# Two residual layers chosen per batch row: the opening of the kernel on TensorE's side rewritten, and one copy at its end moved

## The reference

```
w = weights[subjects]; b = bias[subjects]
out = einsum('bct,bcd->bdt', x, w) + b[:, :, None]
x = x + out
H = einsum('btd,od->bto', x, W)
delta = einsum('btr,bor->bto', einsum('btd,brd->btr', x, A[idx]), Bm[idx]) * scalings[idx]
x = x + H + delta
```

## Time and profile before

| | |
|---|---|
| median of 3 runs | 241.67 us (241.47 to 241.75) |
| the profiled execution | 241.36 us |
| its span in the trace | 239.6 us |
| TensorE matmul / weight load busy | 229.4 us (96%) / 187.7 us (78%) |
| VectorE, ScalarE, GpSimd busy | 149.2, 107.9, 79.6 us |
| DMA | 36.64 MB, mean 153 GB/s |

### The profile page before, as it was taken

One profiled execution on the slowest core, in us unless ns is written; L12 is line 12 of the kernel. 1 busy time (PEld: TensorE's weight loads), 2 busy tenths in 40 slices (PEclk: granted clock), 3 DMA queues, 4 the chain that ended last, 5 costly groups with the idle time before them and its releaser, 6 DMA issues.

```text
span 239.6 us, 9653 instructions
## 1 busy us (share of the span) xinstructions
PE 229.4 (96%) x2900; PEld 187.7 (78%) x2901; DVE 149.2 (62%) x259; ACT 107.9 (45%) x185; POOL 79.6 (33%) x277
## 2 busy tenths in 40 slices
PE   1899999999999999999999999999999999999992
PEld 1787878888887888888888888888788888888761
DVE  6799848873358636875258835875448754425762
ACT  3184663543436363562436354454435434344441
POOL 4467771700077610610056730525135131000000
PEclk9999999999999999999999999999999999999998
DMA  5956455736565474645555574645646364562233
GB/s 132 279 169 193 141 176 156 198 94 176 148 197 141 120 213 131 201 108 192 134 154 163 147 215 109 192 115 160 172 135 191 109 200 110 155 178 63 83 78 90
DMA packets 23723, 36.64 MB, mean 153 GB/s; under 512 B 6162, under 2 KB 6162, under 8 KB 23698
## 3 DMA queue, kind: packets, MB, share of 16 engines
q1 hardware_dynamic: 16480, 26.10, 40.0%
q10 hardware_dynamic: 7218, 10.23, 13.7%
HBM read 19.53 MB, written 16.78 MB: 152 GB/s over the span
## 4 chain that ended last, share of the span: by engine, by line
PE 89%; DVE 2%; DMA 2%; ACTq 2%; issue 1%; ACT 1%; DVEq 0%
PE ps L883 69%; PE ps L843 14%; PE ps L819 3%; DMA o_ring<-in_L_cond_W_dram 2%; PE ps L764 1%; ACTq L693 1%; PE ps L775 1%; DVE o_ring L554 1%; ACT x_hi L658 1%; ACT m_f L681 1%; DVE x_lo L534 0%; PE ps L813 0%; DVE last_parts L539 0%; PE ps L871 0%; DVE o_ring L549 0%
## 5 line engine op out<-in xcount | busy, mean ns | idle before, releaser
L883 PE MATMUL ps<-m_hi,x_hi 128*128 x244 | 97.0, 398 | 0.0
L883 PE MATMUL ps<-m_hi,x_lo 128*128 x244 | 95.1, 390 | 0.0
L883 PE MATMUL ps<-m_lo,x_hi 128*128 x244 | 95.1, 390 | 0.0
L534 DVE TENSOR_TENSOR x_lo<-x,x_hi 128x512 fp32r<-128x512 f32 x64 | 44.7, 698 | 62.8 <-ACT x_hi L658 62.4
L374 POOL COPY p_pair<-p_all 64x64 f32 x128 | 42.8, 335 | 113.8 <-DVE x L526 96.9
L658 ACT ACTIVATE x_hi<-x 128x512 fp32r<-128x512 f32 x64 | 40.4, 632 | 56.0 <-ACT o_ring L671 30.9
L671 ACT ACTIVATE o_ring<-ps 128x512 f32<-128x512 f32 x60 | 35.9, 598 | 52.1 <-PE ps L883 50.7
L883 PEld LDWEIGHTS ps<-m_hi,x_hi 128*128 128x128 f32 x244 | 45.8, 188 | 10.7 <-issue 0.4
L883 PEld LDWEIGHTS ps<-m_hi,x_lo 128*128 128x128 f32 x244 | 45.8, 188 | 9.7
L883 PEld LDWEIGHTS ps<-m_lo,x_hi 128*128 128x128 f32 x244 | 45.8, 188 | 9.0
L526 DVE TENSOR_TENSOR x<-ps,bias_pair 128x512 f32<-128x512 f32 x64 | 43.6, 685 | 11.1 <-PE ps L843 10.1
(11 more groups left out here) (102 smaller groups left out, 82.4 us busy)
## 6 DMA issues: line engine op xcount, KB each, us to landing
x_ring<-in_x_dram SPq DMA_DIRECT2D x122, 128.0 KB, 2.7
out_dram<-o_ring ACTq DMA_DIRECT2D x64, 128.0 KB, 2.6
out_dram<-o_ring SPq DMA_DIRECT2D x64, 128.0 KB, 2.3
a_f<-in_L_cond_A_dram SPq DMA_DIRECT2D x8, 128.0 KB, 2.7
x_ring<-in_x_dram ACTq DMA_DIRECT2D x6, 128.0 KB, 3.4
o_ring<-in_L_cond_W_dram SPq DMA_DIRECT2D x2, 256.0 KB, 4.7
o_ring<-in_L_cond_W_dram ACTq DMA_DIRECT2D x2, 256.0 KB, 5.8
b_nat<-in_L_cond_Bm_dram ACTq DMA_DIRECT2D x1, 256.0 KB, 3.7
```

Source lines behind the costliest of these rows:

```text
L534: nc.vector.tensor_tensor(x1_lo[:, u % HELD], x1[:, u % 2], x1_hi[:, u % HELD], ALU.subtract).then_inc(x1_lo_ready, 1)
L883: mm = nc.tensor.matmul(ps[:, 2 + u % 2, :], part, m_tile(m, k, c), start=(c == 0 and part is hi and m is m_hi), stop=(c == TC - 1 and par ...
```

## The change

The edits, in the order of the program:

- The bias is no longer spread by DMA. GpSimd zeroes a tile `bias_row` of 128 x 512, SP loads the bias into its first row, TensorE multiplies it from the left by the 128 x 128 tile of ones (four fp32 products of 128 columns into bank 0), and ScalarE copies the bank to `bias_all`. SP's load of it stands between W's first and second block, and waits for the zeroing.
- `w` is loaded before W's first block.
- TensorE gets three bf16 products of 512 columns whose result nobody reads (`keep_busy`), between the counting products and the sum of the order. The first turn of W's block 0 moves behind the tables.
- ScalarE zeroes the rows of `a_parts` for the first adapter, GpSimd those for the second, behind the fourth pair.
- SP loads both halves of pairs 2 and 3; ScalarE loads those of pairs 0 and 1 only, with one table word read at a time.
- ScalarE copies chunks 0 to 2 of `wt`, VectorE chunk 3, behind its split of A. ScalarE rounds A of the second adapter behind its load of pair 7.
- Layer 0 of pair 3 moves behind layer 1 of pair 0. At the end, ScalarE copies the first row's low part of the last pair between the copies and the store of the pair before.

```diff
         def _(sp):
...
+            sp.dma_start(p_all[0:C], w.rearrange("s c d -> c s d")).then_inc(w0_in, 16)
             sp.dma_start(w_nat[:, 0, :], W[0:P, :]).then_inc(w_in[0], 16)
-            sp.dma_start(p_all[0:C], w.rearrange("s c d -> c s d")).then_inc(w0_in, 16)
+            sp.wait_ge(bias_zeroed, 1)
+            sp.dma_start(bias_row[0:1, :], bias.rearrange("s d -> (s d)").rearrange("(a n) -> a n", a=1)).then_inc(bias_in, 16)
             sp.dma_start(w_nat[:, 1, :], W[P:2 * P, :]).then_inc(w_in[1], 16)
...
-            b = words(sp, regs[:5], batch[0:1, 2:7], B - 1)
-            for i in range(1, XR):
-                load_half(sp, i, 0, b[2 * i - 2], x_first[i])
+            b = words(sp, regs, batch[0:1, 0:2 * XR], B - 1)
+            load_half(sp, 1, 0, b[2], x_first[1])
+            for i in range(2, XR):
+                load_x(sp, i, b[2 * i:2 * i + 2], x_first[i])
             load_a(1, 1)
             load_quad(XR)
...
-            for half in range(2):
-                nc.gpsimd.memset(a_parts[GR - GR * half:P - GR * half, half, :].bitcast(F32), 0.0).then_inc(rows_zeroed, 1)
-                pool.wait_ge(rows_zeroed, half + 1)
+            nc.gpsimd.memset(bias_row[:], 0.0).then_inc(bias_zeroed, 1)
...
-                    pool.wait_ge(bias_in, 16)
+                    pool.wait_ge(bias_ready, 1)
...
+                if n is None and j == HEAD - 1:
+                    pool.wait_ge(pair_ready, j * 4 + 4)
+                    nc.gpsimd.memset(a_parts[0:GR, 1, :].bitcast(F32), 0.0).then_inc(rows_zeroed, 1)
...
-            dve.wait_ge(wt_turned, 1)
-            nc.vector.tensor_copy(wt[:, 0, :], ps[:, FIRST, :]).then_inc(wt_copied_too, 1)
             a_split(0, 0)
+            dve.wait_ge(wt_turned, TC)
+            nc.vector.tensor_copy(wt[:, TC - 1, :], ps[:, FIRST + TC - 1, :]).then_inc(wt_copied_too, 1)
             x1_add(0, 0)
...
-            act.dma_start(bias_all[:], bias.rearrange("s d -> (s d)").rearrange("(a n) -> a n", a=1)
-                          .to_broadcast([P, S * C]).rearrange("p (s d) -> p s d", s=S)).then_inc(bias_in, 16)
...
+            def copy_last_low(j, u):
+
+                act.wait_ge(out_ready, j)
+                with act.If_ne(last_places[MIXED - 1][0], last_places[MIXED - 1][1]):
+                    copy_low_half(j, u, 0)
...
+            nc.scalar.activation(a_parts[GR:P, 0, :].rearrange("p (c k) -> p c k", c=TC), ones[GR:P, :].unsqueeze(1)
+                                 .to_broadcast([GR, TC, P]), ACT.Copy, scale=0.0).then_inc(rows_zeroed, 1)
             act.wait_ge(batches_ready, 1)
-            b = words(act, last_regs, batch[0:1, 0:2 * XR], B - 1)
-            for i in range(XR):
-                load_half(act, i, 1, b[2 * i + 1], x_first[i])
+            b, = words(act, regs[:1], batch[0:1, 1:2], B - 1)
+            load_half(act, 0, 1, b, x_first[0])
+            act.wait_ge(bias_spread, 1)
+            nc.scalar.activation(bias_all[:].rearrange("p s d -> p (s d)"), ps[:, 0, :], ACT.Copy).then_inc(bias_ready, 1)
+            b, = words(act, regs[1:2], batch[0:1, 3:4], B - 1)
+            load_half(act, 1, 1, b, x_first[1])
             a_round(0, 0)
+            copy_wt(0)
             copy_wt(1)
             copy_wt(2)
-            copy_wt(3)
...
-            a_round(1, 1)
             x1_round(1, 1)
             act.wait_ge(l0_done, XR)
             load_x(act, XR - 1, b, x_in)
+            a_round(1, 1)
...
                     copy_low(j, u)
+                    if j == PAIRS - 2:
+                        copy_last_low(j + 1, u + 1)
                     store_odd(j, u, last_batches[2 * n_of_mixed(j) + 1])
...
+            def spread_bias(part):
+
+                cols = slice(part * P, part * P + P)
+                return nc.tensor.matmul(ps[:, 0, cols], ones[:], bias_row[:, cols], start=True, stop=True)
+
+            def keep_busy(bank, times):
+
+                for _ in range(times):
+                    nc.tensor.matmul(ps[:, bank, :], ident_b[:], ident_b[:].unsqueeze(1).to_broadcast([P, TC, P]),
+                                     start=True, stop=True)
+
+            keep_busy(FIRST, 3)
...
-            for j in range(1, L0_QUAD):
+            for j in range(1, L0_QUAD - 1):
                 first_inputs(j)
                 layer0(j, j)
...
                     layer1_first(k[0])
+                    first_inputs(L0_QUAD - 1)
+                    layer0(L0_QUAD - 1, L0_QUAD - 1)
```

More of the change, by code:

```diff
@@ L671, in copy_out, with copy_low_half @@
                 nc.scalar.activation(o_ring[:, u % OR, :], ps[:, 2 + u % 2, :], ACT.Copy).then_inc(out_ready, 1)
+            def copy_low_half(j, u, half):
+                i = n_of_mixed(j)
+                act.wait_ge(low_done[half][i], 1)
+                nc.scalar.activation(low[0:C, half], ps[C:2 * C, 2 + 2 * half + u % 2, :],
+                                     ACT.Copy).then_inc(low_ready, 1)
             def copy_low(j, u):
@@ L678, in copy_low @@
                 with act.If_ne(last_places[i][0], last_places[i][1]):
-                    for half in range(2):
-                        act.wait_ge(low_done[half][i], 1)
-                        nc.scalar.activation(low[0:C, half], ps[C:2 * C, 2 + 2 * half + u % 2, :],
-                                             ACT.Copy).then_inc(low_ready, 1)
+                    for half in range(2) if j < PAIRS - 1 else (1,):
+                        copy_low_half(j, u, half)
                 with act.Else():
@@ L783, in _ @@
             nc.tensor.matmul(ps[:, 6, 0:K], ones[0:1, :], scal_row[:], start=True, stop=True).then_inc(scal_spread, 1)
-            pe.wait_ge(w_in[0], 16)
-            for c in range(TC):
-                turn_w(0, c)
+            pe.wait_ge(bias_in, 16)
+            for part in range(2):
+                spread_bias(part)
             pe.wait_ge(place_ready, 1)
@@ L794, in _ @@
             mm.then_inc(others_tabled, 1)
+            for part in range(2, TC):
+                mm = spread_bias(part)
+            mm.then_inc(bias_spread, 1)
+            pe.wait_ge(w_in[0], 16)
+            for c in range(TC):
+                turn_w(0, c)
+            turn_b(0)
             pe.wait_ge(w_in[2], 16)
@@ L807, in m_product_first @@
             def m_product_first(chunk):
-                if chunk == 0:
+                if chunk == TC - 1:
                     pe.wait_ge(wt_copied_too, 1)
                 else:
-                    pe.wait_ge(wt_copied, chunk)
+                    pe.wait_ge(wt_copied, chunk + 1)
                 nc.tensor.matmul(ps[:, FIRST + chunk, :], a_parts[:, 0, chunk * P:chunk * P + P], b_parts[:],
```

9 lines of the change are left out of this document (7 added, 2 removed).

## The result

The changed kernel takes **243.52 us** (median of 6 runs, 242.89 to 244.69) where the kernel before takes 241.53 (6 runs beside it, 241.25 to 241.75). The ratio is 1.0078, 95% interval 1.0063 to 1.0094: slower by 0.8%, some 1.9 us. The forecast was 241.3, its range 240.6 to 242.4. The profiled execution took 243.34 us, its span is 241.7; before they were 241.36 and 239.6. So 2.0 us are to be found between the two traces.

What follows compares the result with a forecast made beforehand. TensorE was taken to bound the kernel, carrying 89% of the chain. With -0.8 us at the end and +0.4 in the opening, -0.4 in all, the median was forecast at 241.3 us, range 240.6 to 242.4.

Steps and rivals of the forecast that it cites:

- the quad: Start of layer 0 of pairs 4 to 7, where the opening ends: 22.3 us forecast against 21.90, 0.4 us lost.
- The end, -0.8: Last pair: only the second low-part copy stays before the last addition; 0.8 us gained, at least 0.5, at most 0.85.
- The turns end at 11.2: Opening: TensorE finishes its transposes of W and B at 11.2 us, against 11.93 before.
- if the bias has landed: Condition in the opening: half the bias products, ahead of the tables, cost nothing once the bias row is there.
- tables after 7.2: Sign against the prediction: tables were expected to start at 6.7 to 6.8 us; later than 7.2 means wrong.
- the clock's rise at 9: Opening: gapless earlier TensorE work brings the rise to 2.4 GHz to 9 us, between 8.3 and 12.3.
- Layer 1 of pair 0 at 15.0: Opening: VectorE's chain and the loads both let this layer start at 15.0 us, 0.45 earlier than before.
- SP's loads hold it: Opening: pair 2's second half lands at 14.4 us; with its layer 0, layer 1 of pair 0 waits until 14.95.
- From there 7.3 us to the quad: From layer 1 of pair 0 to layer 0 of pairs 4 to 7: 22.3 us, set by pair 7's load; 6.46 us before.
- The zeroing edits at nothing: Zeroing of rows by ScalarE and GpSimd in the opening costs nothing while their cover holds.
- The bias did come late: Rival, chance 0.13: a late bias row delays tables to 7.6 us and x loads by 0.9, giving 242.4.
- No earlier rise: Rival, chance 0.17: the clock does not rise earlier, transposes end at 12.7 us, opening +1.1, giving 242.0.

Runs made afterwards that it cites:

- e1: Kernel before with only the end's edit (last pair's first low part copied ahead of the store of pair 62): 240.84 us, ratio 0.9958.
- e12: The changed kernel run and traced once more, unchanged: 243.33 us, ratio 1.0076 to the kernel before.
- e11: Changed kernel with bias products made from one row of ones and the one bias row instead of 128 x 128 tiles: 244.70 us, ratio 1.0117.
- e4: Kernel before plus the three products that nobody reads: 241.59 us, ratio 0.9993.
- e10: Changed kernel with layer 0 of pair 3, x loads and rounding of the second A as before, without unread products: 244.87 us, ratio 1.0140.
- e5: Changed kernel with B turned ahead of W's block 0, right behind the bias products: 243.13 us, ratio 1.0065.
- e2: Changed kernel with layer 0 of pair 3 back ahead of layer 1 of pair 0: 242.85 us, ratio 1.0045.
- e8: Changed kernel with the second A rounded ahead of the load of pair 7, as before: 243.43 us, ratio 1.0079.
- e7: Kernel before with only layer 0 of pair 3 moved behind layer 1 of pair 0: 242.66 us, ratio 1.0043.
- e3: Changed kernel with all four bias products behind the tables: 243.11 us, ratio 1.0051.
- e6: Changed kernel without the three products that nobody reads: 242.92 us, ratio 1.0049.
- e9: Kernel before plus eleven small unread products (22 TensorE instructions) ahead of the sum of the order: 242.40 us, ratio 1.0042.

## Why the prediction was wrong

The profiled execution was forecast at 240.96 and took 243.34, 2.4 us more. Of these, 1.43 are at the quad (22.3 forecast, 23.73 measured), 0.90 in the twelve products behind it, and 0.07 at the end. Step by step, as it put them:

**The end, -0.8: right.** It is -0.73, within the 0.5 to 0.85 given, and for the reason given: only the second copy is left between TensorE's end and the last addition. e1 has it alone.

**The turns end at 11.2: wrong, 12.24, and 12.93 in e12.** This step had two parts. The first half of the bias products was to cost nothing "if the bias has landed". It had not: TensorE waited for the row until 6.59, and the second half began at 8.22 where the forecast had 7.1. In the first trace these 1.1 us are the whole miss. By the prediction's own signs, tables after 7.2 meant that it is wrong: they came at 7.81. The second part, the clock's rise at 9, came at 10.3 there (B's transposes 319 ns on average) and at 11.8 in e12 (421 ns). Both lie between the two ends that the prediction gave (8.3 and 12.3), but that the change moves the rise forward at all is not shown (the table of e11), and the unread products, part of the reason given, have no effect that the runs can see (e4, e10). The Trainium skill, TensorE: Matmul & The Clock Gate, Part 4 (PE-mode transpose), has the rule that transposes don't count as busy work, which the prediction set aside. The traces don't settle it: in e11 the engine does little but transposes from 9.11 to 13.89 and stays at the low level throughout, which speaks for it; the kernel before rises at 12.2 after the same kind of work from 7.82 on, and e1 at 11.0 after it from 7.55 on, which speaks against it.

**Layer 1 of pair 0 at 15.0: wrong, 15.72, and 16.08 in e12.** The prediction counted VectorE's row from its split of A on. It left out what stands ahead of that on VectorE, the rounding and splitting of B (10.80 and 11.53), which begin only when TensorE has turned B. From 10.80 to 15.59 it is seven operations, 4.8 us. With B turned by 10.8 no earlier A helps. It also had TensorE's own path at 13.7, without the way through `m_hi`, `m_lo` and `x_lo`, which is 3.15 us from the end of the turns (e5, e12). This is the first step that failed on the critical path: an earlier start of 0.45 us was to pay for the rest, and the start came 0.3 later than before. That SP's loads hold it (14.95 in the prediction) didn't come to bear in the changed kernel; it did in e2.

**From there 7.3 us to the quad: wrong, 8.01.** The wait was foreseen, but at 22.3 by the load of pair 7. It is `x1_add` that is last (22.45 + 0.69 = 23.14), behind the split of the second A, behind its rounding at 20.77, behind the load of pair 7 at 19.59. Timeline of the changed kernel:

```profile
19.59 1.14 ACTq L255 DMA_DIRECT2D x_ring<-in_x_dram  x2
...
20.77 0.63 ACT L642 ACTIVATE a_parts<-a_f 64x512 fp32r<-64x512 f32 x1 [3.33 <-issue]
...
21.50 0.92 DVE L501 SCALAR_TENSOR_TENSOR a_parts<-a_parts,neg,a_f 64x512 fp32r<-64x512 f32 x1 [1.37 <-ACT a_parts L642]
...
22.45 0.69 DVE L535 TENSOR_TENSOR x<-ps,bias_pair 128x512 f32<-128x512 f32 x1
```

The prediction had this chain too, at 22.1 from a start of 15.0, which with 15.72 is 22.8; hand-overs and a split of 0.92 us instead of 0.7 make 23.14 of it. The same split also held TensorE's two products of the second M (L863) until 22.47, so that they end at 23.20. The rest is the 0.53 us of issue before the quad, where 0.16 stood before; what TensorE does in it no view shows. e8 takes the order on ScalarE back and gets 0.6 us here.

The prediction did count the moved layer 0 of pair 3 in TensorE's line (7.0 us instead of 6.46). What it didn't ask is what the move buys. By its own figures TensorE would have been ready at 13.7 (at 14.2 with that layer 0 still ahead) and VectorE only at 15.0, so the 0.5 us lay in a wait and came out of it. e7 has the move alone: 1.0 us lost at the quad, nothing gained.

**Inside layer 1 of pair 2: not foreseen at all, +0.90.** The prediction ended its count at the quad, "from where the pattern repeats" in its words, and so put what the edits do behind it at nothing. Neither forecast nor rival has the gap, and it is the largest single term of the miss. By the experiments it is not a wait for data. It goes with the number of TensorE's instructions: it stands behind the third product in the changed kernel, e2, e3, e5, e8, e11 and e12, all with 2911 products, and behind the fifth in e6 and e10, with 2908. e9 brings a short one behind the third product of a kernel that had none, with 2911. The kernel before, e1 and e7 (2900 products) and e4 (2903) have no gap there.

That TensorE waits for its own code would fit, but the transfers of instructions don't show it. The views have two queues of that kind, q14 and q8. In the changed kernel TensorE stands still from 26.73 to 27.34; between 26.75 and 27.34 no transfer starts on either, and the next one of q14 starts only behind 27.34, when TensorE has resumed. In e2 none starts between 25.50 and 26.50, around its stop from 25.61 to 26.43, and in e8 none between 26.25 and 27.25, around its stop from 26.41 to 27.16. In e6 there is one on q14 between 27.50 and 27.75, where TensorE resumes at 27.63; in e10 the last on q14 before its stop at 28.72 is at 25.75. The kernel before has one between 24.50 and 24.75 in the same twelve products, and no gap. So the position is shown to go with the count of instructions, while the cause of the stop, and what makes it cost 0.3 us in e9 and 0.5 to 1.1 elsewhere, **stays open**. It wasn't tried to take it away while keeping the bias products.

**The zeroing edits at nothing: stands**, as far as the sum goes: it leaves nothing for them. No run tested them alone.

**The rivals.** The bias did come late (TensorE had it at 6.59, beyond the 6.2 named), and the tables at 7.81 as that rival said (7.6). This rival had the sign, the condition, and nearly the place of the quad (23.4, measured 23.73). Its way there was priced differently: it took the tables and the loads behind them as what leads, and e3, with tables 1.6 us earlier, gains 0.1 at the quad. "No earlier rise" gave 12.7 for the turns, 15.6 for layer 1 of pair 0 and 23.0 for the quad; the first trace has 12.2, 15.72 and 23.73, e12 has 12.93, 16.08 and 24.16. Neither held the gap in the twelve products, and by itself that gap is nearly half of what the changed kernel lost.

## What to carry to other kernels

Before a step is moved behind another, ask what releases the other one: if it is a different engine, the moved step was filling a wait, and moving it puts its whole duration into the line. When a start is held by an engine's row of operations, count that row from its first input, not from the operation the edit touches, and look for a second holder close behind. Take a second trace of the same kernel before a holder is named: here it was another one in the second trace. Count on past the point where "the pattern repeats". And test the parts of a bundle alone: here one edit gained 0.4% and the others together cost 1.2%.

## What the runs showed of the hardware

- The column of the granted clock reads 1.00 while the same fp32 transpose takes 421 ns early and 272 ns later. Durations of one form are the clock to go by here.
- The moment of the rise to the 2.4 GHz level differs between executions of one program: 10.3 and about 11.8 us in the two traces of the changed kernel, about 12.2 and 11.0 in those of before and e1, which have the same opening.
- With bias products of one row instead of 128, in the same place, W's transposes took 424 ns on average instead of 311 (357 in e12), and the runs were slower (1.0117 against 1.0076). Three bf16 products of 512 columns, some microseconds earlier, made no difference that shows (e4: 0.85 us for B's four transposes, at the 1.2 GHz level).
- A product of the bias with 128 columns is two instructions and takes about 0.6 us at the low level: 1.22 and 1.15 us for two (four instructions each).
- A row of 2 KB, issued at 2.78 us behind two larger loads, landed at 5.7 to 6.6 us in the runs, 2.9 to 3.8 us after its issue.
- In a straight run of products TensorE stood still for 0.4 to 0.9 us at a place that moved with the count of its instructions; no transfer of instructions started in the stops of the changed kernel and of e2.
